# Score mask on VectorE from the second turn on, with the early loads and the first turns' order laid out anew

## The reference

```
x = x + attn(layernorm(x)) ;  x = x + ffn(layernorm(x))
attn: q, k, v = x @ w.T, 16 heads of 16;  scores = q.k / 4
      scores = -inf where j - i > 16;  softmax;  (attn v) @ wo.T
ffn:  gate_w, up_w (1024 x 256), down_w (256 x 1024): cubic Catmull-Rom
      interpolation of about 2033 control points each
      down( silu(gate(x)) * up(x) )
```

## Time and profile before

| | |
|---|---|
| median of 3 runs | 592.11 us |
| profiled execution, its own time | 592.29 us |
| its span | 590.6 us |
| PE, PEld busy | 580.1 us, 502.6 us |
| VectorE busy | 503.0 us |
| ScalarE, GpSimd busy | 243.9 us, 208.4 us |
| HBM read, written | 12.35 MB, 4.19 MB |

### The profile page before, as it was taken

The page is one execution under the profiler, slowest core; times in us unless marked ns, Lnnn a source line. Parts: engine busy times, 40 slices in busy tenths (PEclk is TensorE's granted clock), DMA queues, the critical chain, the costliest instruction groups (busy, mean ns, idle before and its releaser), DMA issues.

```text
span 590.6 us, 13712 instructions
## 1 busy us (share of the span) xinstructions
PE 580.1 (98%) x5396; PEld 502.6 (85%) x5396; DVE 503.0 (85%) x1029; ACT 243.9 (41%) x369; POOL 208.4 (35%) x249
## 2 busy tenths in 40 slices
PE   7999999999999999999999999999999999999997
PEld 4576679898898888889898988989888888988997
DVE  3689999988989899899989899999998998886542
ACT  1234543544434334443443444443443444443422
POOL 5543441423432333333242334224232323333432
PEclk9999999999999999999999999999999999999999
DMA  8341421322023121221313111132211212101000
GB/s 250 108 140 59 144 96 65 96 72 73 19 73 109 56 92 36 70 74 57 108 56 108 49 61 56 56 107 74 90 57 53 70 42 73 56 21 37 2 19 19
DMA packets 44416, 42.88 MB, mean 73 GB/s; under 512 B 4544, under 2 KB 43072, under 8 KB 44352
## 3 DMA queue, kind: packets, MB, share of 16 engines
q1 hardware_dynamic: 44352, 41.99, 22.6%
HBM read 12.35 MB, written 4.19 MB: 28 GB/s over the span
## 4 chain that ended last, share of the span: by engine, by line
PE 90%; DVE 6%; issue 1%; DMA 1%; ACT 0%; SPq 0%; POOL 0%; DVEq 0%
PE ring L722 15%; PE ring L723 12%; PE ring L724 12%; PE ring L729 8%; PE ring L804 8%; PE ring L730 7%; PE ring L731 7%; PE pair L772 7%; PE pair L796 5%; PE ring L750 3%; PE ring L713 3%; DVE M L657 2%; DMA POWER<-powers 1%; PE pair L781 1%; DVE X L636 1%
## 5 line engine op out<-in xcount | busy, mean ns | idle before, releaser
L561 ACT ACTIVATE P<-pair 128x800 f32<-128x800 f32 x128 | 105.9, 837 | 129.6 <-PE pair L796 129.3
L722 PE MATMUL ring<-YT,WGUh 128*128 128x256 f32 x512 | 151.5, 296 | 0.5 <-DVE QK L595 0.5
L724 PE MATMUL ring<-YT,WGUl 128*128 128x256 f32 x512 | 144.3, 282 | 0.0
L723 PE MATMUL ring<-YT,WGUh 128*128 128x256 f32 x512 | 144.1, 281 | 0.0
L657 DVE TENSOR_REDUCE M<-pair 128x2 f32<-128x288 f32 (+1 forms) x256 | 134.1, 569 | 3.6
L517 POOL TENSOR_TENSOR IN<-GU,IN 128x512 fp32r<-128x512 f32 x64 | 83.3, 1303 | 142.3 <-ACT IN L522 142.2
L722 PEld LDWEIGHTS ring<-YT,WGUh 128*128 128x128 f32 x512 | 96.3, 188 | 7.4 <-issue 2.3
L723 PEld LDWEIGHTS ring<-YT,WGUh 128*128 128x128 f32 x512 | 96.6, 189 | 0.0
L509 POOL TENSOR_SCALAR_AFFINE_SELECT P<-P 128x448 f32<-128x448 f32 x64 | 37.7, 588 | 165.9 <-ACT P L561 165.8
L724 PEld LDWEIGHTS ring<-YT,WGUl 128*128 128x128 f32 x512 | 96.2, 188 | 0.0
L651 DVE TENSOR_TENSOR pair<-pair,UP 128x512 f32<-128x512 f32 x104 | 71.5, 687 | 8.3 <-PE pair L772 7.9
(11 more groups left out here) (80 smaller groups left out, 1074.6 us busy)
## 6 DMA issues: line engine op xcount, KB each, us to landing
QM<-QK SPq DMA_DIRECT2D x96, 128.0 KB, 2.1
KS<-QK SPq DMA_DIRECT2D x96, 128.0 KB, 2.1
X<-x SPq DMA_DIRECT2D x32, 256.0 KB, 2.9
out<-X SPq DMA_DIRECT2D x16, 256.0 KB, 2.3
OVER<-over SPq DMA_DIRECT2D x4, 256.0 KB, 7.4
P<-wqk SPq DMA_DIRECT2D x2, 256.0 KB, 4.3
TAP<-points SPq DMA_DIRECT2D x2, 256.0 KB, 5.4
POWER<-powers SPq DMA_DIRECT2D x2, 256.0 KB, 6.1
```

Source lines behind the costliest of these rows:

```text
L561: nc.scalar.activation(P[:, g % 2, 2 * (n % 2):2 * (n % 2) + 2, :], pair(what, t, n)[:, :, 0:SW], ACT.Exp, scale=SCALE).then_inc(exp_done, 1)
L722: mm(o, wh[:, kb, c], act[:, 0, kb, :], start=j == 0 and kb == 0, stop=False, skip_group_check=True)
L723: mm(o, wh[:, kb, c], act[:, 1, kb, :], start=False, stop=False, skip_group_check=True)
L724: i = mm(o, wl[:, kb, c], act[:, 0, kb, :], start=False, stop=False, skip_group_check=True)
```

## The change

It sets `EARLY` to 1: turns 1 and 2 lose their `mk` steps, and VectorE masks there. It replaces the tables `START`, `OWN[0]`, `OWN[1]` and `OWN[2]`; turns 3 to 15 keep theirs. It loads the tokens of turn 1 within `raw`, each of the two token tiles has a semaphore of its own, and `x` of later turns waits for `zt` of two turns before alone. The mask is loaded after the second piece and not last, `wv` and `wo` come later, and `hot` has 26 matmuls where it had 20.

```diff
-EARLY = 3
+EARLY = 1
 (tables START and OWN[0..2] written anew; the order that they give, up to the first steps of turn 0's scores:)
-fill0 hot0 fill1 la0 lb0 raw tap0 fill2 wj0 split0 zt0 wj1 fill3 ws0 tap1 qk0.0 ws1 split1 ws2 tap2 wj2 wj3 ws3 tap3
- wj4 ws4 la1 ws5 x1 wj5 lb1 ld0.0 fill4 wj6 qk0.1 zt1 x2 split2 ws6 s1 0.0 mk0.0 s1 0.1 mk0.1
+hot0 x1 fill0 raw fill1 la0 lb0 x0 tap0 split0 zt0 fill2 wj0 ws0 tap1 ws1 split1 la1 ld0.0 x2 wj1 qk0.0 tap2 ws2
+ wj2 wj3 ws3 lb1 wj4 fill3 wj5 ws4 zt1 tap3 qk0.1 ld0.1 split2 wj6 ws5 s1 0.0 s1 0.1 mk0.0 mk0.1
...
-ident_loaded, mask_loaded, rows_loaded, x_loaded = map(sem, (
-    "ident_loaded", "mask_loaded", "rows_loaded", "x_loaded"))
+ident_loaded, mask_loaded, rows_loaded = map(sem, ("ident_loaded", "mask_loaded", "rows_loaded"))
+x_loaded = [sem(f"x_loaded{i}") for i in range(2)]
...
-                        if j == 0:
+                        if j == PIECES[0]:
                             sp.dma_start(ROWS[:], ...)
                             query_key(1)
                         sp.dma_start(OVER[:, c], over[:, c]).then_inc(over_loaded[j], DMA)
-                        if j == 0:
+                        if j == PIECES[1]:
+                            sp.dma_start(X[1][:], tokens(x, 1)).then_inc(x_loaded[1], DMA)
+                            for dst, src in ((UP, upper), (IDB, identb)):
+                                sp.dma_start(dst[:], src).then_inc(mask_loaded, DMA)
+                        elif j == PIECES[2]:
                             sp.dma_start(raw(2, 1), wv...)
-                            sp.dma_start(raw(3, 1), wo...)
-                    for dst, src in ((UP, upper), (IDB, identb)):
-                        sp.dma_start(dst[:], src).then_inc(mask_loaded, DMA)
-                elif what == "x" and t:
-                    if t >= 2:
-                        sp.wait_ge(zt_made, nth("zt", t - 2, 0))
-                    if t:
-                        sp.wait_ge(norm_done[0], nth("lb", t - 1, 0))
-                    sp.dma_start(X[t % 2][:], tokens(x, t)).then_inc(x_loaded, DMA)
+                    sp.dma_start(raw(3, 1), wo...)
+                elif what == "x" and t >= 2:
+                    sp.wait_ge(zt_made, nth("zt", t - 2, 0))
+                    sp.dma_start(X[t % 2][:], tokens(x, t)).then_inc(x_loaded[t % 2], DMA)
...
-                        dve.wait_ge(x_loaded, DMA * (t + 1))
+                        dve.wait_ge(x_loaded[t % 2], DMA * (t // 2 + 1))
...
-                    for i in range(20):
+                    for i in range(26):
                         mm(bk[:, 0:S], KS[:, 0, 0, 0:128], KS[:, 0, 1, :], start=True, stop=True)
```

More of the change, by code:

```diff
@@ L100, in steps @@
     return [(what, n + by * i, at + gap * i) for what, n, count, by, at, gap in table for i in range(count)]
-START = [("fill", 0, 1, 1, -415.818, 0), ("hot", 0, 1, 1, -415.817, 0), ("fill", 1, 1, 1, -313.266, 0),
-             ("raw", 0, 1, 1, -223.498, 0), ("tap", 0, 1, 1, -192.468, 0),
[14 rows of a table removed]
-OWN = {0: [("la", 0, 1, 1, -258.964, 0), ("lb", 0, 1, 1, -228.564, 0), ("zt", 0, 1, 1, -187.18, 0),
[62 rows of a table removed]
+START = [("hot", 0, 1, 1, -364.378, 0), ("fill", 0, 1, 1, -303.492, 0), ("raw", 0, 1, 1, -291.644, 0),
+             ("fill", 1, 1, 1, -246.012, 0), ("tap", 0, 1, 1, -169.867, 0),
+             ("split", 0, 1, 1, -160.121, 0), ("fill", 2, 1, 1, -117.523, 0),
[6 rows of a table added]
+             ("tap", 3, 1, 1, -23.5, 0), ("split", 2, 1, 1, -22.566, 0), ("wj", 6, 1, 1, -20.895, 0),
[5 rows of a table added]
+OWN = {0: [("la", 0, 1, 1, -237.809, 0), ("lb", 0, 1, 1, -226.831, 0), ("x", 0, 1, 1, -198.11, 0),
[58 rows of a table added]
        3: [("x", 0, 1, 1, -70.709, 0), ("la", 0, 1, 1, -58.129, 0), ("lb", 0, 1, 1, -44.634, 0),
@@ L423, in _ @@
                 if what == "raw":
-                    sp.dma_start(X[0][:], tokens(x, 0)).then_inc(x_loaded, DMA)
+                    sp.dma_start(X[0][:], tokens(x, 0)).then_inc(x_loaded[0], DMA)
                     sp.dma_start(ID[:], ident).then_inc(ident_loaded, DMA)
@@ L438, in _ @@
                         sp.dma_start(OVER[:, c], over[:, c]).then_inc(over_loaded[j], DMA)
-                        if j == 0:
-                            sp.dma_start(raw(2, 1), wv.rearrange("(k p) c -> p k c", p=128)).then_inc(raw_loaded[2], DMA)
-                            sp.dma_start(raw(3, 1), wo.rearrange("(k p) c -> p k c", p=128)).then_inc(raw_loaded[3], DMA)
-                    for dst, src in ((UP, upper), (IDB, identb)):
-                        sp.dma_start(dst[:], src).then_inc(mask_loaded, DMA)
-                elif what == "x" and t:
-                    if t >= 2:
-                        sp.wait_ge(zt_made, nth("zt", t - 2, 0))
-                    if t:
-                        sp.wait_ge(norm_done[0], nth("lb", t - 1, 0))
-                    sp.dma_start(X[t % 2][:], tokens(x, t)).then_inc(x_loaded, DMA)
+                        if j == PIECES[1]:
[3 more added lines that the diff above has]
+                        elif j == PIECES[2]:
+                            sp.dma_start(raw(2, 1), wv.rearrange("(k p) c -> p k c", p=128)).then_inc(raw_loaded[2], DMA)
+                    sp.dma_start(raw(3, 1), wo.rearrange("(k p) c -> p k c", p=128)).then_inc(raw_loaded[3], DMA)
+                elif what == "x" and t >= 2:
+                    sp.wait_ge(zt_made, nth("zt", t - 2, 0))
+                    sp.dma_start(X[t % 2][:], tokens(x, t)).then_inc(x_loaded[t % 2], DMA)
                 elif what == "ld":
```

## The result

The changed kernel takes 600.46 us (599.42 to 602.0, four runs). The kernel before took 591.97 us beside it (590.9 to 595.0, four runs). The ratio is 1.0151, 95% interval [1.012, 1.0181]: slower. The forecast was 596 us, slower. The direction came true and the time lies in the range given (589.5 to 601), but it is 8.5 us up instead of 4. Single executions of one kernel differ by several us (those of the kernel before, over all runs, lie between 588.4 and 597.6), so medians are compared. The profiled execution took 600.36 us with a span of 598.5.

A forecast was written before the change was run, and what follows sets the result against it. VectorE bounds the front with PE in balance, PE the rest. 11.5 us of masks less 4.5 from the start put `s1` 3.1 at 107.6 and `sc` 2.1 at 107.7; 486.7 follow: span 594.4, time 596 us, range 589.5 to 601.

The forecast's parts named there:

- What bounds the kernel: VectorE full from 34 to 112 us with PE close to full, two engines in balance; PE always busy from about 90 us.
- Part 1: Turns 1 and 2: PE loses 16 `mk` steps, 3.8 us less, at most 5.1.
- Part 2: Turns 1 and 2: VectorE gains 16 mask operations, 1.68 us a masked step, 11.5 us more in all.
- Part 3: New order of turns 0 to 2: neutral for VectorE up to `s1` 3.1; PE has 1.2 us less behind `sc` 2.1.
- Part 4: The start: 4.5 us gained from VectorE's 14.4 us of waits, bounds 0 and 7.5; changed loads priced at 0.
- The start: Before the first scores: these come at 29 to 30 us instead of 33.97, giving back 4.5 us.
- The distance: From `s1` 3.1's maximum to `sc` 2.1 on PE: about 2 us before, forecast at 107.6 and 107.7 us.
- Reordering moves nothing out of VectorE's way: Up to `s1` 3.1 VectorE's steps stay the same except `ga` 0.3 in, `wo` 1.0 out, 0.6 us each way.
- rival B: VectorE not the limit, 584 us, chance 0.14; counter-argument: 5.0 us of start waits are first tokens and `POWER`, which no order shortens.
- PE's weight loads: Sign of being right: thinner than before between 40 and 100 us, with waits on VectorE's maxima.
- A: Rival: the clock rises early during `hot`, halving the start's PE work; start gives 7.5 us, 593 us, no change, chance 0.26.
- C: Rival: the start gives nothing, PE waits as before and masks cost in full; 600.6 us, chance 0.14.

The follow-up runs named there:

- p1_old_no_mask: Kernel before with the mask of turns 1 and 2 left out on every engine, its `mk` steps removed too: 590.8 us, ratio 0.9994.
- e2_old_dve_mask: Kernel before with `EARLY` = 1 alone, so VectorE masks turns 1 and 2 in the old tables, loads and start unchanged: 603.86 us, ratio 1.0193.
- e1_new_pe_mask: Changed kernel (new tables and loads) with `EARLY` = 3, so PE masks turns 1 and 2 again: 597.19 us, ratio 1.0084 to the kernel before.
- h3_new_start_old_own: The change's `START`, loads and 26 `hot` with the old `OWN` tables of turns 0 to 2, PE masking: 620.85 us, ratio 1.0489 to the kernel before.
- e6_old_hot26: Kernel before with 26 `hot` matmuls alone: 590.65 us, ratio 0.9988.

## Why the prediction was right in direction and wrong in size

*What bounds the kernel.* Right in the main: VectorE's work counts up to 112 us, PE alone behind it. The rows of 200 to 300 us are unchanged. In the old order 3.8 us less on PE gives 1.0 us (`p1_old_no_mask`) and the masks on VectorE cost in full (`e2_old_dve_mask`), so the front hangs on VectorE more than "in balance" says.

*Part 1, 3.8 us off PE.* The amount is about right (by the table of losses PE's own work fell from 590.6 - 28.4 = 562.2 to 598.5 - 39.9 = 558.6 us), its worth in the front is small; the sum gave it no credit there.

*Part 2, 11.5 us on VectorE.* Right: 1.69 us a step, and 11.4 to 12.1 us of time in the old tables.

*Part 3 and Part 4, what the new order and start give back.* This is the step that failed. My sum had them return 7.7 us of the 11.5 (4.5 in the start, 2.0 by PE's distance to `sc` 2.1, 1.2 by less work behind it). They return 2.5 to 3.4 by `e2_old_dve_mask` against the changed kernel, and 3.5 by the places that the sum goes by: 2.3 by the start, 0.9 by the distance (2.1 us before, 1.2 after), 0.3 behind it (487.9 us before, 487.6 after). The terms:

- The start: first scores at 30.6 us (before 34.0), near the 29 to 30 forecast; but one spline step that stood ahead of them before (from 32.92 to 33.97, 1.05 us) was still to come, so the gain was 3.4 - 1.05 = 2.3 us, not 4.5. `zt` 1 alone waited 2.40 us for VectorE's `lb` 1. VectorE's waits before 34 us fell from 14.4 to 9.5 us, of which the two slow operations of `lb` 1 took back 3.2.
- The distance: I had `sc` 2.1 start 0.1 us behind the maximum, on the assumption that PE stands ready there. It started 1.2 us behind, since PE had been held at earlier maxima and copies. PE loses time all along from 37 us, not at one place.
- "Reordering moves nothing out of VectorE's way": true of VectorE's list up to `s1` 3.1, but not enough. I compared the lists at one place and by one engine. `e1_new_pe_mask` shows that the new tables by themselves cost 5 us, which my sum didn't have at all; by the table of losses this arises along the whole way and not at one place.

For the first point, the lone spline step ahead of the first scores of the kernel before, and `zt` 1 and the first scores of the changed one:

```profile
32.92 1.12 PE L750 MATMUL ring<-TAP,ROWS 32*128 32x512 f32 x2
```

```profile
24.51 1.09 PE L707 MATMUL ring<-ID,X 128*128 128x128 f32 x4 [2.40 <-DVE X L630]
...
30.59 1.13 PE L766 MATMUL pair<-KS,QM 63*128 63x256 f32 x8
```

How VectorE waited, before 34 us and from 34 to 120 us:

```profile
DVE ST L618 <- DMA X<-x: 3.4, 1, 3.4
DVE ZT L589 <- ACT ZT L516: 2.0, 2, 1.2
```

```profile
DVE QK L589 <- ACT QK L516: 1.2, 2, 0.9
DVE GU L693 <- PE ring L718: 0.7, 1, 0.7
```

The tokens' 3.4 us stand as they did, as rival B's counter-argument had it. From 34 us on VectorE has no air, so its 1.7 us of waits were rightly left standing. PE's weight loads, as forecast, wait for VectorE's maxima; before, that row read 3.0 us, 7 times. Over the whole span:

```profile
PEld pair L766 <- DVE M L651: 9.6, 15, 1.5
```

*The rivals.* A, the clock rising early, came true in part: it read 1.00 up to 16.6 us, then 0.50 until 33.6. It did not give 593 us. B (VectorE not the limit) fell. C's time, 600.6, is what was measured, though not by its mechanism: the start gave something, and the order took it.

*What stays open.* Where the floor of the new tables sits. Against the kernel before, `e1_new_pe_mask` gains 2.6 us up to the first scores, loses 3.8 up to `sc` 0.0 and 3.5 behind it; only about 1 us was moved by an edit, within the noise. `h3_new_start_old_own`, meant to split start from turns, failed to. That the mix of the two engines' work is the cause is argued from the traces, not shown by a run that mends it, and how much of the time without masks is the fall of the clock is open too. No kernel here is better than the one before beyond what can be told: the best medians, 590.65 and 590.8 (the latter without its masks), have 1 inside their intervals.

## What to carry to other kernels

Where two engines are in balance, time the new order with the old work, and the old order with the new work, before adding their prices: here each was slower, 5.5 and 12.1 us, and the two partly covered each other, 8.5 together. When comparing two orders, follow the cumulative work of both engines along the list, not of one engine at one meeting place: a run of steps dear to one and cheap to the other can starve the other (argued here, not shown). Before matmul counts of two kernels are compared, compare their granted clocks. And earlier first scores are a gain only in so far as no other step has been put off behind them.

## What the runs showed of the hardware

Spline matmuls (32 rows, 512 columns) follow the clock, and neighbouring steps overlap. The same lone step, two matmuls, takes 10.55 - 8.58 = 1.97 us in the kernel before and 9.81 - 8.79 = 1.02 us in an execution with 26 `hot` in which the clock was up by then. Two neighbouring steps, four matmuls, take 2.0 us at 1.2 GHz and 1.06 us at 2.4 GHz. The 1.0 us a step at either level, in the expectation of `e6_old_hot26`, sets half of a pair at 1.2 GHz beside a lone step at 2.4. Matmuls of 256 columns went from 0.21 to 0.12 us. The kernel before, and `e6_old_hot26`:

```profile
8.58 2.04 PE L750 MATMUL ring<-TAP,ROWS 32*128 32x512 f32 x2 [1.13 <-DVE TAP L605]
10.55 1.11 PE L713 MATMUL ring<-ID,X 128*128 128x128 f32 x4
```

```profile
8.79 1.09 PE L750 MATMUL ring<-TAP,ROWS 32*128 32x512 f32 x2
9.81 0.65 PE L713 MATMUL ring<-ID,X 128*128 128x128 f32 x4
```

The granted clock can read 1.00 ahead of its first change in the record. Before, has 1.00 at 10 to 20 us beside matmuls 0.21 us apart. In one execution of that kernel with 26 `hot` (`e6_old_hot26`) the record shows it otherwise:

```profile
10.00:20.00 10.00, 9.16 (x30) 4.67 (x29) 6.92 (x10) 3.61 (x6) 2.91 (x3) 0.77 1.02 274
20.00:30.00 10.00, 9.65 (x28) 6.14 (x28) 8.76 (x16) 2.71 (x5) 7.21 (x6) 0.55 0.08 27
...
30.61 0.46 PE L772 MATMUL pair<-KS,QM 63*128 63x256 f32 x4
```

Its clock was at the upper level for some of the time before 19 us, its first scores stood at 30.6 instead of 34.0 us, and this execution took 588.64 us, though the median is that of before. The executions of the kernel before spread from 588.4 us (mean granted clock 0.988) to 597.6 (0.971). That is as large as the effect of the change, and a single profiled execution must be read with it in mind. The moment at which the clock rises is not in the kernel's hand alone; the Trainium skill, "TensorE: Matmul & The Clock Gate", Part 1, says that it varies from run to run, and the clocks of that one kernel's executions agree.

Beside GpSimd's tensor operations and clearings two VectorE operations took 3.97 us instead of 0.73, and taking that away left the median where it was.
